# Gated graph layers on one core: 10 instead of 12 of every 26 quads of edges summed densely, eight gather steps per superblock instead of seven

## The reference

```python
h = jnp.maximum(_layernorm(x, axis=-1), 0.0)
h = h @ lin_w.T + lin_b
for i in range(3):
    m = h @ weight[i]
    agg = jax.ops.segment_sum(m[src], dst, num_segments=n_nodes)
    h = gru_cell(agg, h, w_ih, w_hh, b_ih, b_hh)
return x + h
```

## Time and profile before

| | us |
|---|---|
| median of 3 runs | 5887.51 |
| the 3 runs | 5881.04, 5918.47, 5887.51 |
| the profiled execution, its own time | 5864.06 |
| its span in the profile | 5862.2 |
| prologue and first gathers, until rounds begin | 0 to 235 |
| layer 0 while rounds are counted | 235 to 2820 |
| layer 0's last steps and tiles, until layer 1's first gather | 2820 to 2943 |
| layer 1, first gather to last step's sum on PE | 2943 to 4388 |
| layer 2, the same | 4409 to 5846 |

### The profile page before, as it was taken

How to read it: one execution, slowest core, us unless ns; L and a number is a source line. 1 busy time by engine, 2 the same in 40 slices (tenths; PEclk the granted TensorE clock), 3 DMA queues, 4 the chain that set the end, 5 groups by cost and what they waited for, 6 DMA issues and landing times.

```text
span 5862.2 us, 83667 instructions
## 1 busy us (share of the span) xinstructions
PE 3831.5 (65%) x31796; PEld 2541.3 (43%) x31797; DVE 1824.9 (31%) x7602; ACT 1102.4 (19%) x2163; POOL 3481.9 (59%) x3518
## 2 busy tenths in 40 slices
PE   4255555544455554444358888888875888888887
PEld 3144444433344444333224444544542444444454
DVE  7233434433333443333212222222221222222222
ACT  3133333333333333332100000000010000000000
POOL 5766555666665565665556566565645655656554
PEclk8566666766666666666679999999987999999998
DMA  5545444544445454444546666666664666666664
GB/s 181 153 128 141 139 136 138 148 128 130 135 131 143 140 146 126 137 135 118 171 150 213 204 204 212 209 206 204 217 211 150 211 202 200 210 206 199 204 214 140
DMA packets 726236, 992.59 MB, mean 169 GB/s; under 512 B 74424, under 2 KB 606520, under 8 KB 725816
## 3 DMA queue, kind: packets, MB, share of 16 engines
q1 hardware_dynamic: 471336, 582.73, 30.8%
q0 software_dynamic: 165888, 339.96, 21.2%
q10 hardware_dynamic: 88592, 64.25, 3.6%
HBM read 755.57 MB, written 231.08 MB: 168 GB/s over the span
## 4 chain that ended last, share of the span: by engine, by line
PE 52%; another core or an unknown queue 20%; issue 15%; ACT 5%; DVE 5%; DMA 1%; DVEq 1%; POOL 0%; ACTq 0%; POOLq 0%; SPq 0%
PE psum L758 26%; PE psum L738 9%; PE psum L736 4%; ACT pieces_region L591 4%; PE psum L716 4%; PE psum L704 3%; PE psum L675 1%; PE psum L676 1%; PE psum L677 1%; DVE onehot L1036 1%; DVE pieces_region L1137 1%; PE psum L688 1%; DVE aggT L1073 1%; DVEq L1026 1%
## 5 line engine op out<-in xcount | busy, mean ns | idle before, releaser
L468 POOL DMA_INDIRECT ring_region<-messages,edge_src x3456 | 3421.4, 990 | 2268.5 <-issue 1003.1
L758 PE MATMUL psum<-stage_region,pieces_region 128*128 128x432 f16 x9408 | 1862.7, 353 | 163.4 <-issue 161.6
L738 PE MATMUL psum<-pieces_region,stage_region 128*128 128x112 bf16 (+1 forms) x5376 | 998.4, 268 | 1160.3 <-ACT pieces_region L591 568.8
L758 PEld LDWEIGHTS psum<-stage_region,pieces_region 128*128 128x128 bf16 x9408 | 911.6, 99 | 1039.4 <-issue 317.2
L738 PEld LDWEIGHTS psum<-pieces_region,stage_region 128*128 128x128 bf16 x5376 | 641.0, 121 | 1345.2 <-issue 1266.0
L591 ACT CAST pieces_region<-psum 128x504 f16<-128x504 f32 x1344 | 759.5, 580 | 1830.8 <-remote 1005.8
L1059 DVE TENSOR_TENSOR aggT<-aggT,psum 128x36 f32 x864 | 166.7, 193 | 2741.8 <-remote 1658.7
L736 PE MATMUL psum<-pieces_region,stage_region 128*128 128x112 bf16 (+2 forms) x4032 | 837.8, 276 | 40.6 <-issue 40.4
L716 PE MATMUL psum<-onehot,ring_region 128*128 128x36 bf16 x10368 | 416.0, 184 | 454.4 <-issue 364.9
L716 PEld LDWEIGHTS psum<-onehot,ring_region 128*128 128x128 bf16 x10368 | 367.8, 101 | 537.8 <-issue 463.5
L1036 DVE TENSOR_SCALAR onehot<-iota_block,edge_rel 128x36 bf16<-128x36 bf16 x3456 | 531.1, 252 | 3.2 <-issue 2.9
(11 more groups left out here) (93 smaller groups left out, 1507.3 us busy)
## 6 DMA issues: line engine op xcount, KB each, us to landing
stage_region<-counts SPq DMA_DIRECT2D x448, 768.0 KB
counts<-pieces_region SPq DMA_DIRECT2D x192, 896.0 KB
ring_region<-messages,edge_src POOLq DMA_INDIRECT x3456
pieces_region<-messages SPq DMA_DIRECT2D x21, 1344.0 KB
temps<-states ACTq DMA_DIRECT2D x147, 128.0 KB
messages<-pieces_out ACTq DMA_DIRECT2D x98, 192.0 KB
states<-temps ACTq DMA_DIRECT2D x98, 128.0 KB
messages<-ring_region SPq DMA_DIRECT2D x25, 384.0 KB, 2.9
```

Of the source, the lines that this page charges most:

```text
L468: nc.gpsimd.indirect_dma_start(out=rows[:, n % RING, h * QC + c, :], out_offset=None, in_=messages[layer], in_offset=bass.IndirectOffsetOn ...
L738: mm = nc.tensor.matmul(by_block[:, :, covered:high], blocks_oh[j % 2][:, c, :], x_round[:, :, covered - low:], start=(c == 0), stop=True, ...
L758: mm = nc.tensor.matmul(psum[:, 6 + kg % 2, 0:DQ * W], res[:, b, piece * P:(piece + 1) * P], stage[v % ABUF][:, :, cols], start=(b == 0 an ...
```

## The change

`DQ` goes from 12 to 10. With it GQ goes from 14 to 16, GSB from 7 to 8 steps per superblock, the steps of layers 1 and 2 from 112 to 128 each, the quads with counts from 192 to 160, the rounds of layer 0 from 1344 to 1120, the columns of each dense matmul from 432 to 360, and one slice of counts from 768 KB to 640 KB. The number of dense matmuls (4704 a layer), of steps in layer 0 (208) and of tile updates stays. `stage_region` gets the larger of the counts' buffers (20,480 bytes a partition) and the planning arrays (22,528 bytes); before, the buffers were the larger (24,576).

```diff
@@ -13,7 +13,7 @@
 QE = QC * P
 W = 36
 SQ = 26
-DQ = 12
+DQ = 10
 GQ = SQ - DQ
 HB = 7
 SLW = 256
@@ -137,7 +137,7 @@
         aggT = sb("aggT", [P, AGG])
         PB = max(NB * MW * 2, NPAD * 4 + 2 * PRO * PTN * 4 + 8 * P + 4 * RW)
         region = sb("pieces_region", [P, PB // 4])
-        SBYTES = ABUF * DQ * SLW * 2
+        SBYTES = max(ABUF * DQ * SLW * 2, 4 * NQ * (QC + 8) + 4 * NSB * DQ * QC)
         stage_r = sb("stage_region", [P, SBYTES // 4])
         ring_r = sb("ring_region", [P, RING * 8 * MW // 2])
         temps = sb("temps", [P, 10 * TN])
```

## The result

The change made the kernel slower: 6170.9 us (6135.5 to 6196.6) against 5895.4 us (5881.0 to 5918.5), ratio 1.046, 95% interval 1.040 to 1.052. Forecast were 5517 us, in a range from 5380 to 5720. Within a group of runs all repetitions agree within about 1%. I call them *stalling* and *clean* chips, for a reason that the traces show, and compare total times only within a group. The six groups after the first have six different chip numbers on record (that of the first isn't recorded), and none came twice, so a property of the chip can't be told from one of the moment.

A forecast was written before the change was run, and what follows sets the result against it. The prediction took PE as the bound, in layer 0 PE and ACT together, with POOL ahead. 5864.1 - 251 (layer 0) - 2 x 60 (layers 1 and 2) = 5493 us, 5517 on the median's scale; range 5380 to 5720.

The forecast's parts named there:

- What bounds the kernel: Whole kernel: PE sets the end, in layer 0 with ACT; POOL is ahead, waiting 762.8 us for PE's sums.
- I take 10.6, as if two of eight steps paid that 2.4 us: Layers 1 and 2: a step takes 10.6 us, between 10.03 without waits and 12.56 as before.
- the upper end 12.56: Layers 1 and 2: upper bound per step, unchanged at 12.56 us, making a layer 1636 us (+190).
- The term of -60 us a layer: Layers 1 and 2: 128 x 10.6 + 28 = 1385 us a layer, 60 us less than 1445.
- Rival A: Layers 1 and 2: steps keep 12.56 us, set by POOL and its hand-over; +201 us a layer, 6038 us; 10%.
- demonstrably runs at 10.03 when buffers are free: Layers 1 and 2: POOL's undisturbed step is 10.03 us, from 40 gathers 1.254 us apart; reason for choosing near the low end.
- PE's price of the width: Layers 1 and 2: 360 columns save PE 155 us, added sums cost 15.5 us; PE alone gains 139.5 us a layer.
- 164.7: Layers 1 and 2: dense matmul time in ns at 360 columns, 32.9 ns less than 197.6 (0.165 us in the prediction).
- 224 rounds x 1.12 us = 251 us: Layer 0: 224 fewer rounds, each worth 1.12 us, save 251 us; ends 155 and 365 us.
- my lower bound of 0.69: Layer 0: lowest price of a round, 0.69 us from PE's own busy time, 155 us for 224 rounds.
- The rule weighed against the change: Dense matmuls: Trainium skill's issue-gap page makes 72 columns worth some 9 ns, 44 us a layer, 5579 us in all.
- The median as a base: Whole kernel: the runs' median, 5887.5 us, 23.4 above the profiled execution, used to move 5493 to 5517 us.

The follow-up runs named there:

- the narrow variant: Kernel before, still 112 steps a layer, each dense matmul streaming 360 instead of 432 columns (some sums left out): 5766.8 us, ratio 0.998, on a stalling chip.
- the variant that would have told (5399 us): Kernel before, POOL waiting for the previous step's rows only after a step's first gather: 5399.2, 5389.9, 5392.6 us, ratios 1.134, 1.131, 1.132, clean chips.

## Why the prediction was wrong

*What bounds the kernel: half right.* On a stalling chip PE practically never waits for rows, as said. But POOL's waits aren't the measure of PE's lateness that I took them for: of the kernel before's 178 pauses over 3 us 96 end within 0.85 us of the PE sum that frees the buffer, of the changed kernel's 198 only 76. In the others the sum was done and its update came late. Wrong, too, was to read PE's idle time as a fixed loss beside PE's own work. It answers to PE's speed. Where PE is early enough for the update to come in time, the gathers run unbroken, PE stalls until POOL fills the ring and stops, and what PE gained is gone; where the update comes late, POOL pauses 3.5 us. The step is 12.3 to 12.8 us with 12 or 10 dense quads, 432 or 360 columns, and with a forced pause 12.7 to 12.9. That both effects go with gathers is shown by the layers without them; why they add up to nearly the same step isn't derived.

*Layers 1 and 2: the step that failed.* "I take 10.6, as if two of eight steps paid that 2.4 us", against the upper end 12.56 from the earlier trace rows. Measured over the gathers of each layer are 12.40 and 12.36 us a step. Not two of eight steps paid for a pause but more than six: 198 of 244 boundaries took over 3 us, and the mean boundary was 3.55 us (3.72 in the kernel before) where 1.25 is the one without a pause. The term of -60 us a layer came out as +172 and +164. Rival A, given 10%, had the right account as far as it went, that the step's length belongs to POOL and its hand-over: it said +201 a layer, and its condition (a step over 12.0 us) was met. Its remark that "the pause is there although PE isn't late by much" is what the updates show. The sentence that led me off was that POOL "demonstrably runs at 10.03 when buffers are free". POOL did, but PE stood nearly still beside those 40 gathers (16 matmuls in 33 us, above), so they never showed a pace that both engines can keep. The row was in front of me in the earlier trace rows as well, eight gathers beside 23 matmuls in 13 us, right where two steps' gathers had met without a pause.

*PE's price of the width: right, and worth nothing.* 139.5 us a layer forecast, 136 measured in layer 1 between the two variants without gathers (1136.2 and 1000.4 us from sum to sum). On a stalling chip the narrow variant shows 11 us for the whole kernel. The matmuls' mean rose from 157.6 ns (741.5 / 4704) without gathers to 183.8 ns (864.4 / 4704) in the changed kernel, as the granted clock was 0.83 there and 0.98 without gathers (157.6 x 0.98 / 0.83 = 186); I had 164.7.

*Layer 0: sign right, size a quarter.* The term was 224 rounds x 1.12 us = 251 us; the last sum of layer 0 came 63 and 72 us earlier after its first (2704 against 2767, 2716 against 2787). That is 0.3 us a round, below my lower bound of 0.69, PE's own busy time for it. A bound from busy time holds only where the time set free is used. Here it probably went into stalls again: layer 0's unbroken boundaries rose from 56 to 91. POOL's waits fell from 556 to (316.8 + 143.8) = 461 us in the build's window, and the gathers' own spacing rose from 1.354 to 1.381 us. On clean chips a removed round is worth nothing: layer 0 took 2281 us with 1120 rounds and 2260 with 1344, on two of them.

*The rule weighed against the change.* The trace and PE's 29.6 ns for 72 columns without gathers (187.2 less 157.6) stand by 0.41 ns a column. The 9 ns worked out from the Trainium skill's "TensorE: Matmul & The Clock Gate", section "Back-to-back issue gap", isn't borne out; the sum didn't hang on it.

*The median as a base.* The kernel before took 4763 to 5895 us depending on the chip. The relative result moved far less, 1.042 to 1.064.

No version beat the kernel before. A ring of more than four buffers, by which POOL could learn of a free buffer earlier, wasn't run; by the table it might only make longer runs and more stalls. More dense quads is the direction that saves steps, but on a clean chip PE's 1115 to 1136 us a layer already equals POOL's 112 x 10.2 = 1142, and PE would need some 140 us more at 14 quads; this wasn't run. At 12 both engines are in balance there.

## What to carry to other kernels

Before costing a change that moves work from one engine to another, find what the second engine's operation does to the first at a rate that the trace of before hardly has: sort the first's idle time by the length of the second's unbroken runs, and look at the first engine in the very stretch that shows the second undisturbed. Don't take the name behind a wait for its cause: look when the work that it names had ended. Here a queue that seemed to have 2.6 us of slack in a step of 12.6 had almost none, so that added steps cost nearly their full length and less work for PE gave nothing back. And a probe that removes the suspected disturber (layers without gathers) separates an engine's own price from what the kernel will see of it.

## What was not expected of the hardware

- On stalling chips, while POOL issues indirect gathers, PE's semaphore updates reach ACT, DVE and POOL late (median 3.75 us in layers 1 and 2 of the changed kernel, 0.01 on a clean chip or without gathers), and from about the seventh gather of a run on PE's matmuls come 0.7 to 2.8 us apart. In layer 0 ACT's copies come 2 to 8 us late. The late updates come some 2.7 us after a run's last gather began, PE's full pace some 4.0 us after it. In clean groups runs of over a hundred steps of gathers without a pause don't disturb PE; what it idles there is waiting for rows.
- The updates are a symptom, and which part of the path holds them and PE up, and whether the pause or the empty queue ends it, is open: the variant that would have told (5399 us) only ran on clean chips. A late supply of instructions, as far as the DMA queues show it, isn't it: of the 52 stalls in layers 1 and 2 of the changed kernel's trace, no stall ends within 1 us after a packet of the two queues that the page calls "instruction" has landed, and 45 see none of the larger queue begin.
- The same binary differs by 1100 us, 23%, between chips (5874 and 4771 us), and repeats within 1% on each.
- A pause forced by waiting for a step's last rows costs 3.0 us a step on a clean chip and 1.4 to 1.5 us behind one more gather ((5390 - 4771) / 432 = 1.4).
- TensorE's granted clock followed PE's gaps: 0.98 in a layer without gathers, 0.91 with them, 0.86 with narrower matmuls, 0.83 in the changed kernel, each with PE less busy than the one before.
